# A convolution and attention kernel: the values' 3x3 running sum kept in PSUM, in half slabs, with five sum banks for TensorE

## What is computed

```python
kv = einsum('oc,bchw->bohw', qkv_w, x)       # 1x1 projection to keys and values
kv = dw3x3(kv, qkv_conv_w)                   # a 3x3 filter of its own for each channel
k, v = split(kv, 2, axis=1)
q = idwt2(dw3x3(ll), dw3x3(lh), dw3x3(hl), dw3x3(hh))   # of the wavelet transform of x
attn = softmax(normalised(q) @ normalised(k).T * temperature)   # 8 heads of 16 channels
out = proj_w @ (attn @ v)
```

## Time and profile before

| | |
|---|---|
| median of 3 runs | 1521.6 us (1512.75 to 1523.82) |
| the profiled execution's own time | 1522.41 us |
| its span from first to last instruction | 1520.8 us |
| mean granted TensorE clock | 0.895 |
| PE busy | 1217.5 us (80%) |
| DVE busy | 1130.7 us (74%) |
| ACT busy | 803.3 us (53%) |
| POOL busy | 417.4 us (27%) |

### The profile page before, as it was taken

The page is one execution under the profiler, slowest core; times in us unless marked ns, Lnnn a source line. Parts: engine busy times, 40 slices in busy tenths (PEclk is TensorE's granted clock), DMA queues, the critical chain, the costliest instruction groups (busy, mean ns, idle before and its releaser), DMA issues. The chain is left out here.

```text
span 1520.8 us, 35362 instructions
## 1 busy us (share of the span) xinstructions
PE 1217.5 (80%) x12644; PEld 969.6 (64%) x12644; DVE 1130.7 (74%) x1643; ACT 803.3 (53%) x1382; POOL 417.4 (27%) x241
## 2 busy tenths in 40 slices
PE   0999756888899798988889988954699999799910
PEld 0555456888898797988888888941355555455500
DVE  6777358899999999999999999914776673153384
ACT  0677654656666465665565565511134425666473
POOL 6100032246283544643835427012000000000000
PEclk9999966889899898998998989975899999899965
DMA  9966862433434343443434343125877632000059
GB/s 328 415 270 276 257 150 67 117 97 104 128 92 117 89 117 83 120 110 96 133 83 120 83 121 83 51 66 212 295 272 249 208 88 84 0 1 1 0 232 404
DMA packets 148696, 221.18 MB, mean 145 GB/s; under 512 B 115624, under 2 KB 116788, under 8 KB 144192
## 3 DMA queue, kind: packets, MB, share of 16 engines
q1 hardware_dynamic: 137456, 152.26, 32.8%
q0 software_dynamic: 6480, 47.19, 8.2%
q10 hardware_dynamic: 4608, 19.67, 3.8%
HBM read 131.84 MB, written 87.20 MB: 144 GB/s over the span
## 5 line engine op out<-in xcount | busy, mean ns | idle before, releaser
L874 DVE SCALAR_TENSOR_TENSOR b_vacc<-b_vin,b_vtaps,b_vacc 128x1152 f32<-128x1152 f32 x256 | 430.9, 1683 | 0.0
L1596 PE MATMUL b_conv_bank<-b_sign,wsign 128*128 (+1 forms) x1728 | 295.7, 328 | 10.3 <-ACT b_sign L1376 7.7
L833 ACT CAST b_feat<-b_bank 96x400 f16<-96x400 f32 x255 | 125.0, 490 | 288.9 <-PE b_bank L917 288.8
L915 PE MATMUL b_bank<-b_yh,b_tmh 96*96 96x200 f16 x768 | 204.8, 267 | 71.0 <-DVE b_yl L880 61.8
L1596 PEld LDWEIGHTS b_conv_bank<-b_sign,wsign 128*128 128x128 bf16 x1728 | 168.2, 97 | 140.2 <-issue 27.4
L915 PE MATMUL b_bank<-b_tkh,b_kt 96*96 96x100 f16 x1536 | 247.4, 222 | 3.4 <-DVE b_tml L896 3.3
L916 PE MATMUL b_bank<-b_tkl,b_kt 96*96 96x100 f16 x1536 | 246.4, 221 | 0.0
L917 PE MATMUL b_bank<-b_tkh,b_kt 96*96 96x100 f16 x1536 | 245.9, 221 | 0.0
L675 POOL TENSOR_TENSOR b_xl<-b_xraw,b_xh 96x1536 f16<-96x1536 f32 x32 | 121.5, 3797 | 365.6 <-ACT b_xh L798 365.6
L915 PEld LDWEIGHTS b_bank<-b_tkh,b_kt 96*96 96x96 f16 x1536 | 211.0, 137 | 4.9 <-DVE b_tml L896 3.5
L917 PEld LDWEIGHTS b_bank<-b_tkh,b_kt 96*96 96x96 f16 x1536 | 210.4, 137 | 0.0
(11 more groups left out here) (209 smaller groups left out, 2447.3 us busy)
## 6 DMA issues: line engine op xcount, KB each, us to landing
b_vin<-value_projection_scratch SPq DMA_DIRECT2D x32, 686.0 KB, 5.3
keys_scratch<-b_khl SPq DMA_DIRECT2D x24, 784.0 KB, 3.5
value_projection_scratch<-b_vout ACTq DMA_DIRECT2D x24, 784.0 KB, 4.6
b_kt<-keys_scratch SPq DMA_DIRECT2D x128, 147.0 KB, 2.8
b_xraw<-in_x SPq DMA_DIRECT2D x128, 144.0 KB, 4.8
values_scratch<-b_vacc SPq DMA_DIRECT2D x32, 576.0 KB, 3.2
b_values<-values_scratch SPq DMA_DIRECT2D x48, 384.0 KB, 3.8
out<-xs SPq DMA_DIRECT2D x25, 576.0 KB, 7.0
```

The lines of the kernel that those rows point to most:

```text
L833: nc.scalar.copy(*target(n, 0, k)).then_inc(s_hi, 1)
L874: nc.vector.scalar_tensor_tensor(acc, src, vtaps[:, t:t + 1], acc, ALU.mult, ALU.add).then_inc(s_tap, 1)
L915: nc.tensor.matmul(out, w_hi, m_hi, start=first, stop=False)
L1596: ins = nc.tensor.matmul(cbank[k % NBK][:, 0:CH].rearrange("p (r c) -> p r c", c=W), p["wsign"][nth // NIMG][:, t * C:(t + 1) * C], padded ...
```

## The change

The running sum of a slab goes to two PSUM banks (`vsum`), which the ring of sum banks gives up: `NB` is 5. Two banks hold 2 x 512 floats for each channel and the slab has 1152, so the slab is done in two halves of 6 rows (576 columns, 288 in each bank), each with its taps 1 to 8: 16 operations m = 0 to 15 for each slab in place of 8. Tap 1 of a half reads `vin` and `vacc` in SBUF and writes PSUM; taps 2 to 7 read `vin` and PSUM and write PSUM; tap 8 reads `vin` and PSUM and writes `vacc` in SBUF. They stand behind all jobs except 2, 7, 12 and 17: m = 0 is behind job 0, m = 8 (tap 1 of the second half) behind job 10, m = 15 behind job 19.

```diff
-        NB = 7
+        NB = 5
+        HALF = SLAB // 2
         bank = [ctx.enter_context(nc.psum_tensor(f"b2_bank{i}", [C, 512], F32)) for i in range(NB)]
         gbank = ctx.enter_context(nc.psum_tensor("b2_gram", [C, 512], F32))
+        vsum = ctx.enter_context(nc.psum_tensor("b2_value_sum", [C, 2, 512], F32))
...
-        TAPS = [1, 3, 6, 8, 11, 13, 16, 18]
+        NO_TAP = (2, 7, 12, 17)
...
-                sp.wait_ge(s_tap, i * 8 + 8)
+                sp.wait_ge(s_tap, i * 16 + 16)
...
-            def tap(k, i, t):
-
-                slot = k % 2
-                src = vin[:, slot, :].rearrange("p (r c) -> p r c", c=WP)[:, t // 3:t // 3 + SLAB, t % 3:t % 3 + W]
-                acc = vacc[:, slot, :].rearrange("p (r c) -> p r c", c=W)
-                if t == 1:
+            def tap(k, i, m):
+
+                slot, half, t = k % 2, m // 8, m % 8 + 1
+                src = vin[:, slot, :].rearrange("p (r c) -> p r c", c=WP)[:, half * HALF + t // 3:(half + 1) * HALF + t // 3,
+                                                                          t % 3:t % 3 + W]
+                src = src.rearrange("p (b r) c -> p b r c", b=2)
+                whole = vacc[:, slot, half * HALF * W:(half + 1) * HALF * W].rearrange("p (b r c) -> p b r c", b=2, c=W)
+                part = vsum[:, :, 0:HALF // 2 * W].rearrange("p b (r c) -> p b r c", c=W)
+                if m == 0:
                     dve.wait_ge(s_tap0, i + 1)
-                else:
-                    dve.wait_ge(s_tap, i * 8 + (t - 1))
-                nc.vector.scalar_tensor_tensor(acc, src, vtaps[:, t:t + 1], acc, ALU.mult, ALU.add).then_inc(s_tap, 1)
+                if m or not isinstance(i, int) or i:
+                    dve.wait_ge(s_tap, i * 16 + m)
+                nc.vector.scalar_tensor_tensor(whole if t == 8 else part, src, vtaps[:, t:t + 1], whole if t == 1 else part,
+                                               ALU.mult, ALU.add).then_inc(s_tap, 1)
...
             def body(k, i, pairs, how):
-                t = 1
+                m = 0
                 for n in range(J):
                     if active(n, how):
                         dve.wait_ge(s_hi, i * J + (count(n, how) + LEAD))
                         low(n, k)
-                    if n in TAPS:
-                        tap(k, i, t)
-                        t += 1
-                assert t == 9, t
+                    if n not in NO_TAP:
+                        tap(k, i, m)
+                        m += 1
+                assert m == 16, m
```

## The result

| | median | runs |
|---|---|---|
| kernel before | 1518.56 us (1512.75 to 1523.82) | 9 |
| changed kernel | 1508.76 us (1503.89 to 1514.3) | 9 |
| ratio | 0.9934, 95% interval 0.9908 to 0.9959 | |

What follows compares the result with a forecast made beforehand. DVE was taken as the bound, PE close behind. From 1522.4 us: +38 halves, -19 stretch, -6 idle, +1 last step gave 1536 us; less 6 us for POOL's `null_parts`, 1530 us on the median's level. Range 1486 to 1575 us.

Steps and rivals of the forecast that it cites:

- What bounds the kernel: In the changed block DVE sets the pace at 24.6 us a step, of which 20.8 us pure work; PE close behind.
- Rival E: Taps were never the bound; PE at 21.3 us of 23.5 sets the pace, nothing changes, 1522 us; chance 0.05.
- Halves: Eight DVE taps a step become sixteen half taps of 0.74 us each: 1.2 us more a step, +38 us.
- Rival D: PSUM operands in place cost more: 0.07 us a half tap, 1566 us, or a second pass, 1760 us; chance 0.08.
- Which operations collide: Only tap 1 of each half can still meet POOL; of the 72 us stretch 53 us stay, -19 us.
- 23 x 2.3 = 53 us, and the term falls by 19 us: Stretch left at m = 8 beside POOL's L675: 23 steps at 2.3 us, nine counted as free.
- twelve of 31 steps: Steps of the old kernel where POOL starts more than 0.48 us behind job 10; nine of them counted as free.
- the last step: In the block's last step taps stand next to each other and wait for their predecessor: +1 us.
- POOL's earlier x: POOL's `null_parts`, hardly disturbed now, no longer delays the x that PE waits for: 6 us taken off.
- Idle time and ring: Five banks spread PE's waits, new one at `s1` 16; DVE's idle stays 50 us, less 6 us.
- B: m = 8 gets ahead of POOL's L675 everywhere, so the whole stretch goes: 1477 us; chance 0.27.
- C: m = 8 waits 2.5 us for POOL in all 32 steps, half clock adds 5 us: 1573 us; chance 0.22.

Runs made afterwards that it cites:

- the short `low_x`: POOL's `low_x` cut from 1536 to 96 elements for each partition, in both kernels: 1427.39 us for the kernel before, 1464.32 us for the changed one.

## Why the prediction was right and wrong

**What bounds the kernel** stood. Pure work is what the account leaves over, so its sum proves nothing by itself; but it came out at 645 us in every kernel with eight taps a step (702 with `low_x` on DVE, 57 us more) and at 674 to 677 us in every one with sixteen. Rival E, that taps are not the bound, falls with the 37 us between the two kernels with the short `low_x`.

**Halves.** 0.74 us a half tap, +38 us, was forecast; 0.72 us and +31 us were measured (20.8 to 21.8 us a step). Small, and the right choice between far bounds: with the sum in PSUM the half tap is 806 ns, in SBUF 804. The 0.96 elements a ns don't come out of the rows that the prediction names (from the 504-wide split to the tap, 648 elements and 0.73 us, it is 0.89), but the runs bear them out: 1402 ns for the tap and 804 for its half in SBUF are 598 ns for 576 elements. Rival D is out. The Trainium skill (VectorE: DVE Perf Modes, the TRN2 errata) states 58 fixed cycles from SBUF and 120 from PSUM, an estimate of 65 ns more; the trace does not agree, with 804 ns in SBUF against 806 in place in PSUM and 798 from PSUM to SBUF.

**Which operations collide.** Right: taps 2 to 8 are free, as the splits were. The rule of the Trainium skill on two SBUF inputs (SBUF — State Buffer, "Who interferes with whom") is borne out by 821 against 3009 ns. Right too that m = 8 would run into `low_x` in some steps and not in others, and that `null_parts` and L684 would not matter for DVE.

**The step that failed is the size of the stretch that stays**: "23 x 2.3 = 53 us, and the term falls by 19 us". It is 16 x 1.96 = 31 us, and the term fell by 41. Three quarters of the error (7 x 2.3 us) is the count. I called a step free only where POOL had started over 0.48 us behind job 10, and took nine of them; fifteen are free. Seven of these are of the kind that I meant, with POOL behind m = 8. The other eight are steps such as 10, where POOL is on record 0.2 to 0.3 us ahead of m = 8 and yet the tap goes first. The step that the prediction worked through, with POOL's row at 667.86 us, is one of them: I put m = 8 at 0.3 us behind POOL's start, it came 0.2 us behind (at 663.06 against 662.87 us), and it was not delayed. I had taken "on record first" for "first", on the evidence of old taps that waited 2.75 us with POOL only 0.1 us ahead. The rest is the wait: POOL is done 3.1 us after its start, so a tap that comes 1.0 us later waits some 1.9 us; the 2.75 us of the old kernel did not carry over.

The "twelve of 31 steps" was a misreading as well: in the trace of the kernel before POOL starts over 0.48 us behind job 10 in fifteen of them. That fifteen is also the number of free steps is chance, for three of them (4, 8 and 20) collided and 10, 16 and 18 were free in their place.

This one term turned the sign: the sum with 41 in place of 19 is 1508 us. That it meets the 1508.8 us measured so closely is in part luck. In that sum the halves and the last step are 8 us too dear, the idle time is 12 us too low (-6, and -6 for POOL's earlier x, against 0), and it starts from 1521.6 us, 3 us above the median of nine runs.

**Idle time and ring.** -6 was forecast, 0 came (46 us in both). I read that as a balance: the ring alone costs 10 us, 9 of them idle time, and less stretch gives idle time back; no run shows the two apart in the changed kernel. Also the 6 us taken off for POOL's earlier x were real in kind: the gaps ahead of splits 3 to 5 that the kernel before has in steps 6 and 22, 4.9 us together, are gone. What the prediction missed was the link between the two terms. Where the stretch went wholly, idle time went with it, 24 us of 46 in the kernel before. In the changed kernel the gaps go with the collisions too: a free step behind a free one has none and takes 21.8 us, a colliding step behind a free one has 0.6 us ahead of m = 8, and the step behind a collision has up to 5.7 us.

**Rivals.** B, no collision at all, was put at 1477 us. It was not what this change does; without collisions the changed kernel takes 1457 us with m = 8 behind job 8 and 1464 us with the short `low_x`, less than B's sum, which left the idle time nearly as it was. C did not come; even with a collision in every step (m = 8 behind job 12) the time was 1503 us.

## What to carry to other kernels

Two vector operands in SBUF beside a busy GpSimd is a resource like any other: count such operations and ask which GpSimd instruction each meets, because the loser waits until the other is done and the engines behind it then wait as well. Moving an operand to PSUM frees all operations but those that still read two SBUF tensors, and for these the order decides; here another order of the half taps was worth five times what the move brought. Before paying banks or doubled instructions for a stall, try what only reorders: an earlier slot, the other engine's work in pieces, or that work on another engine.

## What the runs showed of the hardware

*The collisions cost both sides.* POOL's operations shrank with the change (the groups of the lines, before and after):

```profile
L696 POOL TENSOR_TENSOR b_edge<-b_feat 96x128 f32<-96x128 f16 x32 | 61.2, 1941 | 30.4 <-DVE b_feat L880 30.4
```

```profile
L698 POOL TENSOR_TENSOR b_edge<-b_feat 96x128 f32<-96x128 f16 x32 | 16.5, 543 | 27.5 <-DVE b_feat L886 27.5
```

The same operation takes 543 ns in place of 1941. With the half taps in SBUF it takes 960 ns, so the larger part came with the half taps and their places and the rest with PSUM. Of GpSimd's 417 us (27%), 174 went without any change to its own work, and so were waiting.

*A GpSimd record that starts first does not always go first, and I can't say what decides.* In the kernel before with the short `low_x`, POOL and DVE in step 7:

```profile
379.82 1.07 POOL L675 TENSOR_TENSOR b_xl<-b_xraw,b_xh 96x96 f16<-96x96 f32 x1 [13.20 <-ACT b_xh L797]
```

```profile
379.73 0.56 DVE L879 TENSOR_TENSOR b_feat<-b_bank,b_feat 96x400 f16<-96x400 f32 x1
380.21 0.56 DVE L879 TENSOR_TENSOR b_yl<-b_bank,b_yh 96x400 f16<-96x400 f32 x1
380.69 1.42 DVE L873 SCALAR_TENSOR_TENSOR b_vacc<-b_vin,b_vtaps,b_vacc 128x1152 f32<-128x1152 f32 x1
```

96 elements take POOL 0.36 us in the changed kernel with the same cut. Here they take 1.07 us and end 0.2 us behind the start of the SBUF tap, with only splits on DVE in between. It is the same with the full `low_x` in the 18 steps of the kernel before where it began 0.1 to 1.3 us ahead of the tap that it delayed: it ended 2.93 to 3.03 us behind the start of that tap, whatever its lead, and the tap lost 2.75 us or a little more. Where it had begun 1.6 us or more ahead, the tap lost 1.3 to 1.8 us. In the changed kernel `low_x` runs its 3.1 us from its own start when m = 8 comes 0.7 us or more later, and lets m = 8 pass when it comes up to 0.3 us later. Why the one that is later on record should win there, and why POOL seems held up through splits in one kernel and not in the other, stays open.
